# Three token norms run by quarters of the tokens instead of once over all of them

## What is computed

```
h = patches @ W_lin + b + positions                       # class token in front
h = h + recurrent_attention(layernorm(h))                 # layer 0
h = h + bit_linear_ffn(layernorm(h))                      #   8-bit activations, ternary weights
h = h + softmax_attention(layernorm(h))                   # layer 1
h = h + mixture_of_experts(layernorm(h))                  #   32 experts, router picks 8 per token, 2 shared

layernorm(x) = (x - mean(x)) / sqrt(var(x) + 1e-5)        # over the 256 channels, no weights
```

## Time and profile before

| | us |
|---|---|
| median of 3 runs | 880.58 (880.32 to 883.83) |
| profiled execution | 881.1 |
| its span, first to last instruction | 879.4 |
| PE busy in the span | 793.7 (90%) |
| DVE busy | 614.7 (70%) |
| ACT busy | 391.3 (45%) |
| norm 1, from its first mean to the first product behind it | 22.98 to 44.59 |
| norm 2, likewise | 323.96 to 341.19 |
| norm 4, likewise | 526.40 to 542.65 |

### The profile page before, as it was taken

How to read it: one execution, slowest core, us unless ns; L and a number is a source line. 1 busy time by engine, 2 the same in 40 slices (tenths; PEclk the granted TensorE clock), 3 DMA queues, 4 the chain that set the end, 5 groups by cost and what they waited for, 6 DMA issues and landing times.

```text
span 879.4 us, 19821 instructions
## 1 busy us (share of the span) xinstructions
PE 793.7 (90%) x7700; PEld 586.2 (67%) x7700; DVE 614.7 (70%) x976; ACT 391.3 (45%) x561; POOL 183.5 (21%) x197
## 2 busy tenths in 40 slices
PE   4998978989986988977798998799999999999997
PEld 3665757944543666755487885477777777777775
DVE  5796697678787386898767977767777655545544
ACT  5344764610224143666457965334444432323332
POOL 7000790006999801000402420000000000000000
PEclk9999979999999999999999999799999999999999
DMA  8000000020000000010130001144444322222221
GB/s 310 1 2 1 3 1 3 3 96 1 0 0 1 0 2 1 1 39 1 37 78 14 22 21 38 57 127 158 154 150 154 109 68 57 70 69 69 68 61 51
DMA packets 24073, 46.07 MB, mean 52 GB/s; under 512 B 2605, under 2 KB 10541, under 8 KB 23629
## 3 DMA queue, kind: packets, MB, share of 16 engines
q1 hardware_dynamic: 24013, 45.21, 16.8%
HBM read 41.91 MB, written 1.36 MB: 49 GB/s over the span
## 4 chain that ended last, share of the span: by engine, by line
PE 70%; DVE 21%; ACT 4%; issue 3%; POOL 1%; DMA 1%; SPq 0%; DVEq 0%; ACTq 0%; POOLq 0%
PE psum L1790 11%; PE psum L1791 11%; PE psum L1792 11%; PE psum L1982 6%; PE psum L1992 4%; PE psum L828 4%; PE psum L829 4%; PE psum L830 4%; PE psum L2124 1%; DVE arena L1460 1%; PE psum L2170 1%; DVE arena L1658 1%; PE psum L1963 1%; PE psum L2187 1%; PE psum L2156 1%
## 5 line engine op out<-in xcount | busy, mean ns | idle before, releaser
L1790 PE MATMUL psum<-xh,arena 128*128 128x296 f16 (+1 forms) x664 | 193.3, 291 | 8.3 <-DVE xl L1333 5.0
L1791 PE MATMUL psum<-xl,arena 128*128 128x296 f16 (+1 forms) x664 | 193.2, 291 | 0.0
L1792 PE MATMUL psum<-xh,arena 128*128 128x296 f16 (+1 forms) x664 | 193.2, 291 | 0.0
L697 DVE TENSOR_TENSOR arena<-arena 128x592 f16<-128x592 f32 x68 | 52.7, 775 | 61.1 <-ACT arena L608 60.8
L603 ACT ACTIVATE arena<-psum 128x592 f32<-128x592 f32 x66 | 43.8, 664 | 115.7 <-PE psum L1792 115.7
L1790 PEld LDWEIGHTS psum<-xh,arena 128*128 (+2 forms) x664 | 65.3, 98 | 30.8 <-DVE xl L1333 4.5
L752 DVE TENSOR_TENSOR arena<-psum,arena 128x592 f32<-128x592 f32 x64 | 49.6, 775 | 50.8 <-PE psum L1792 50.6
L828 PE MATMUL psum<-arena 128*128 128x296 f16 x272 | 79.9, 294 | 4.6 <-DVE arena L697 3.8
L608 ACT ACTIVATE arena<-arena 128x592 f16<-128x592 f32 x66 | 46.0, 696 | 77.6 <-DVE arena L691 74.8
L829 PE MATMUL psum<-arena 128*128 128x296 f16 x272 | 79.9, 294 | 0.0
L830 PE MATMUL psum<-arena 128*128 128x296 f16 x272 | 79.8, 293 | 0.0
(11 more groups left out here) (321 smaller groups left out, 1675.3 us busy)
## 6 DMA issues: line engine op xcount, KB each, us to landing
arena<-comb SPq DMA_DIRECT2D x62, 296.0 KB, 3.3
arena<-in_wmoe SPq DMA_DIRECT2D x34, 384.0 KB, 3.0
arena<-in_xt SPq DMA_DIRECT2D x4, 864.0 KB, 9.6
arena<-in_w SPq DMA_DIRECT2D x2, 1024.0 KB, 6.6
arena<-arena SPq DMA_DIRECT2D x6, 187.0 KB
arena<-in_ctrl SPq DMA_DIRECT2D x1, 1056.0 KB, 9.1
out<-arena SPq DMA_DIRECT2D x2, 512.0 KB, 3.1
arena<-in_wlin SPq DMA_DIRECT2D x1, 768.0 KB, 4.4
```

What stands on the lines that cost most here:

```text
L697: dve.tensor_tensor(al[:, s_], t1, ah[:, s_], ALU.subtract).then_inc(ev["al"], 1)
L1790: pe.matmul(dst, wh, mh, start=start, stop=False)
L1791: pe.matmul(dst, wh, ml, start=False, stop=False)
L1792: return pe.matmul(dst, wl, mh, start=False, stop=stop)
```

## The change

For ln1, ln2 and ln4 the new `norm_by_quarters` gives each quarter a mean, a variance, a root, a reciprocal and a spreading of its own. In round r the engines do: the product of quarter r, the mean of quarter r-1, the variance of r-2, the spreading of r-3, and (on DVE) the last step of r-4. So a quarter's root and reciprocal run while later quarters are still projected. ln3 keeps the old form.

The tile shapes change. A quarter's 296 sums now lie as 4 rows (`PARTS`) of 74 columns (`PART`) in its own 32 partitions: eight matmuls of 74 columns, each with a slice of `mean_comb` (one column of 1/256 among zeros) that puts its sums into row x. Root and reciprocal are then 32 x 74 (rows 4 to 31 hold zeros from the sums). Spreading takes four matmuls of 74 columns a quarter, with a column of `ident`, broadcast 128 wide, that picks row x.

In the diff the first of the three functions is ACT's, the second DVE's, the third PE's. The 16 fillers before the spreading and, in ln1, the 12 before `condition` are gone; 4 stand before the last spreading in ln2 and ln4. The fillers of the work that follows ln2 (18) and ln4 (12) stay. The small inputs of ln1 go into round 2, the two weight splits of ln4 into round 5.

```diff
+PARTS = 4
+PART = CH // PARTS
...
+            def norm_by_quarters(name, split=True):
+                if name != "ln2":
+                    act.activation(warm[:, int(name[2]) - 1:int(name[2])], eps[:, 0:1], ACT.Sqrt)
+                for r in range(1, NCH + 3):
+                    if 0 <= r - 2 < NCH:
+                        q = r - 2
+                        rows = slice(32 * q, 32 * q + 32)
+                        full(act, (name, "v", q))
+                        act.activation(sd[rows, 0:PART], bank((name, "v", q))[rows, 0:PART], ACT.Sqrt,
+                                       bias=eps[rows, 0:1]).then_inc(emptied["act"], 1)
+                    if r - 1 < NCH:
+                        q = r - 1
+                        after(act, (name, "m", q))
+                        act.activation(sq[:, :, cols(q)], xc[:, :, cols(q)], ACT.Square).then_inc(ev[name + "_sq"], 1)
+                    if 0 <= r - 3 < NCH:
+                        q = r - 3
+                        after(act, (name, "r", q))
+                        if split:
+                            act.activation(xh[:, :, cols(q)], xc[:, :, cols(q)], ACT.Copy).then_inc(ev[name + "_xh"], 1)
...
+            def norm_by_quarters(name, lead, last, extra):
+                for r in range(NCH + 4):
+                    if r < NCH:
+                        lead(r)
+                    if 0 <= r - 1 < NCH:
...
+                        dve.tensor_tensor(xc[:, :, cols(q)], hT[:, :, cols(q)], mean, ALU.subtract).then_inc(emptied["dve"], 1)
+                    if 0 <= r - 2 < NCH:
...
+                        dve.reciprocal(sd[rows, 0:PART], sd[rows, 0:PART]).then_inc(ev[name + "_rec"], 1)
+                    if 0 <= r - 3 < NCH:
...
+                    if 0 <= r - 4 < NCH:
+                        last(r - 4)
+                    if r in extra:
+                        extra[r]()
...
-            norm("ln1", lead=tok_lead, meanwhile=small_inputs)
+            norm_by_quarters("ln1", tok_lead, low_part("ln1"), {2: small_inputs})
...
-            norm("ln4", lead=turned_back, meanwhile=last_lows)
+            norm_by_quarters("ln4", turned_back, low_part("ln4"), {5: last_lows})
...
+            def norm_by_quarters(name, source, lead):
+                for r in range(NCH + 3):
+                    if r < NCH:
+                        lead(r)
+                    if 0 <= r - 1 < NCH:
...
+                    if 0 <= r - 2 < NCH:
+                        q = r - 2
+                        ps = fill((name, "v", q))[32 * q:32 * q + 32, 0:PART]
+                        pe.wait_ge(ev[name + "_sq"], q + 1)
+                        for x in range(PARTS):
+                            comb = mean_comb[:, PARTS - 1 - x:PARTS - 1 - x + 32]
+                            at = CH * q + PART * x
+                            pe.matmul(ps, comb, sq[:, 0, at:at + PART], start=x == 0, stop=False)
+                            ins = pe.matmul(ps, comb, sq[:, 1, at:at + PART], start=False, stop=x == PARTS - 1)
+                        ins.then_inc(filled[who((name, "v", q))], 1)
+                    if 0 <= r - 3 < NCH:
...
+                        if q == NCH - 1 and name != "ln1":
+                            keep_clock(ps, KEEP["quarter"])
+                        pe.wait_ge(ev[name + "_rec"], q + 1)
+                        for x in range(PARTS):
+                            ins = pe.matmul(ps[:, PART * x:PART * x + PART],
+                                            ident[rows, 32 * q + x:32 * q + x + 1].to_broadcast([32, 128]),
+                                            sd[rows, 0:PART], start=True, stop=True)
...
-                if (i, q) == (0, 0):
-                    keep_clock(ps, KEEP["split"])
```

More of the change, by code:

```diff
@@ L104, in norm, with norm_by_quarters @@
             add((name, "r", q), "dve")
-    norm("ln1", lambda q: [add(("tok", c, q), "dve") for c in range(2)])
+    def norm_by_quarters(name, lead):
+        for r in range(NCH + 3):
+            if r < NCH:
+                lead(r)
+            if 0 <= r - 1 < NCH:
+                add((name, "m", r - 1), "dve")
+            if 0 <= r - 2 < NCH:
+                add((name, "v", r - 2), "act")
+            if 0 <= r - 3 < NCH:
+                add((name, "r", r - 3), "dve")
+    norm_by_quarters("ln1", lambda q: [add(("tok", c, q), "dve") for c in range(2)])
     for h in range(2):
@@ L151, in token_max @@
             add((name, "m", n), "act")
-    norm("ln2", lambda q: [add(("op", c, q), "dve") for c in range(2)])
+    norm_by_quarters("ln2", lambda q: [add(("op", c, q), "dve") for c in range(2)])
     token_max("mx1")
@@ L166, in plan_tiles @@
                 add(("v1", n), "dve")
-    norm("ln4", lambda q: [add(("OT", n), "dve") for n in (2 * q, 2 * q + 1)])
+    norm_by_quarters("ln4", lambda q: [add(("OT", n), "dve") for n in (2 * q, 2 * q + 1)])
     add(("lg",), "act")
@@ L277, in tower, with last_in @@
         router_bank = {("lg",): 1, ("cT", 0): 7, ("cT", 1): 0, ("cT", 2): 1}
+        def last_in(b):
+            return [key for key in order[:place[("ln4", "r", 2)][0]] if place[key][0] % 8 == b][-1]
         n0 = place[("f2", 0, 0)][0]
@@ L1089, in _ @@
             act.activation(ctrlh, ctrl_raw, ACT.Copy).then_inc(ev["ctrlh"], 1)
-            norm("ln1")
+            norm_by_quarters("ln1")
             act.wait_ge(ev["dw"], 1)
@@ L1296, in _ @@
                         weight_high(act, e // 2, e % 2, 16 * (e // 2 + 1))
-            norm("ln4")
+            norm_by_quarters("ln4")
             moe_act(act, link)
@@ L1797, in keep_clock @@
                               stop=True)
+            def norm_by_quarters(name, source, lead):
+                for r in range(NCH + 3):
+                    if r < NCH:
+                        lead(r)
+                    if 0 <= r - 1 < NCH:
+                        q = r - 1
+                        after(pe, source(q))
+                        ps = fill((name, "m", q))[:, 0:CH]
+                        pe.matmul(ps, mean_ones[:], hT[:, 0, cols(q)], start=True, stop=False)
+                        pe.matmul(ps, mean_ones[:], hT[:, 1, cols(q)], start=False, stop=True).then_inc(
+                            filled[who((name, "m", q))], 1)
+                    if 0 <= r - 2 < NCH:
+                        q = r - 2
+                        ps = fill((name, "v", q))[32 * q:32 * q + 32, 0:PART]
[6 more added lines that the diff above has]
+                        ins.then_inc(filled[who((name, "v", q))], 1)
+                    if 0 <= r - 3 < NCH:
+                        q = r - 3
+                        rows = slice(32 * q, 32 * q + 32)
+                        ps = fill((name, "r", q))
+                        if q == NCH - 1 and name != "ln1":
[5 more added lines that the diff above has]
+                                            sd[rows, 0:PART], start=True, stop=True)
+                        ins.then_inc(filled[who((name, "r", q))], 1)
             def norm(name, source, lead=None):
@@ L1817, in norm @@
                 ins.then_inc(filled[who((name, "v"))], 1)
-                if name == "ln1":
-                    pe.wait_ge(ev["masks"], 1)
                 keep_clock(fill((name, "r", 0)), KEEP["rec"])
@@ L1838, in tokens @@
                     ins.then_inc(filled[who(("tok", c, q))], 1)
-            norm("ln1", lambda q: ("tok", 1, q), tokens)
+            norm_by_quarters("ln1", lambda q: ("tok", 1, q), tokens)
             pe.wait_ge(ev["condl"], 1)
@@ L2045, in token_max @@
                         ins.then_inc(filled[who((name, kind, n))], 1)
[L2047 removed]
+            norm_by_quarters("ln2", lambda q: ("op", 1, q), out_projection)
             token_max("mx1")
```

34 lines of the change are left out of this document (27 added, 7 removed).

## The result

The changed kernel took 886.39 us (median of 8 runs, 885.50 to 891.04), the kernel before 880.75 on the same chip (8 runs). The ratio is 1.0056, with a 95% interval of 1.0037 to 1.0076. The forecast was 879.4 with a range to 883.6, so the time lies outside it, on the slow side. The profiled execution took 888.99, its span 887.3.

What follows compares the result with a forecast made beforehand. PE was taken to bound the kernel, with 70% of the chain. Norms 1, 2 and 4 at -1.2, +0.5 and -0.4 us made -1.2 with rounding: 881.1 profiled became 879.9, less 0.5 for the median, 879.4 us; range 875.6 to 883.6.

Steps and rivals of the forecast that it cites:

- Norm 1, -1.2 forecast: ln1: PE-bound rounds of 2.9 us, the rotation's second L1416 at about 51.1 instead of 52.28, so -1.2 us.
- the walk: All three norms: PE, DVE and ACT orders followed row by row, each start the later of engine's end and input's hand-over.
- the loop from v2 to v3: Norm 1, sums of squares of quarters 2 to 3: root 2 precedes ACT's square 3, 2.2 us, v3 starting at 40.8.
- Norm 2, +0.5 forecast: ln2: 18 fillers behind the last spreading end last, so the transposes start at 341.67 instead of 341.19, +0.5 us.
- Norm 4, -0.4 forecast: ln4 to the router: Silu starts earlier and L709 starts at 547.9 against 548.33, so -0.4 us.
- Silu 0.4 us earlier: ACT behind norm 4: Silu starts at 545.5 against 545.88, as it no longer waits for `gate_up`.
- Rival 1: Spreading: passes as short as the 74-column transposes, 0.065 instead of 0.11 us, total -3.1, 877.5 us; chance 0.12.
- rival 4: Eight-matmul sums of each quarter: a pass costs a weight load, 0.107 us, total +6.7, 887.3 us; chance 0.10.
- rival 5: Spreading: loads into the same 32 rows stand in the open, 0.17 us a pass, total +2.9, 883.5 us; chance 0.06.
- Rival 2: Behind ln1 or in a norm where fillers went: one more low clock stretch, +1.7 us, 881.1 us; chance 0.18.
- cost nothing: Norm 1: the 28 fillers that go lay beside waits, so their removal was put at no cost.
- masks: Spreading: the wait for `masks` that goes guarded nothing later than DVE's own wait; put at no cost.

Runs made afterwards that it cites:

- ln2_only: Norm 2 alone by quarters, the other norms in the old form with their old fillers, against the kernel before: 887.05 us, ratio 1.0043.
- norm 1 alone: Norm 1 by quarters, norms 2 and 4 in the old form with their old fillers, against the kernel before: 885.15 us, ratio 1.0026.
- the changed kernel on the second chip: The changed kernel, unedited, measured again on another chip against the kernel before there: 886.80 us, ratio 1.0042.

## Why the prediction was wrong

- **Norm 1, -1.2 forecast, +0.2 measured at full clock.** The mechanism (rounds bound by PE, the wait behind the last quarter shorter) is what the rows show. The step that failed is a term that the walk put at nothing: the start of a group of another block. The forecast let PE lose 0.1 only "where PE stood", but PE lost 0.09 to 0.15 at each of the three groups of a round while it was busy, 3.27 instead of 2.90. Mean 2 moved by 1.25 instead of 0.9. A smaller slip: the loop from v2 to v3 was put at 2.2 with a root of 0.27, where the forecast's own root is 0.32; it took 43.86 - 41.43 = 2.43.
- **Norm 2, +0.5 forecast, +2.2 measured.** The same term, on a longer run of groups, twelve changes of block where there were four: PE goes from the sums of quarter 3 through two spreadings, 4 fillers and 18 fillers to the transposes with hardly a stop. That the fillers end last was right, and shown by taking ten away.
- **Norm 4, -0.4 forecast, +0.8 measured.** Again PE without a gap, and twelve changes of block. A second step failed with it: the forecast had Silu 0.4 us earlier "as it no longer waits for `gate_up`". It came 20.6 after the first mean, where it was 19.5 (545.88), and PE's `gate_up` (L1866) was still what it waited for, as before:

```profile
554.25 0.66 ACT L645 ACTIVATE arena<-psum 128x592 f32<-128x592 f32 x1 [0.32 <-PE psum L1866]
```

- **The prices.** Sums 0.066 a pass for 0.064, spreading 0.11 for 0.11, reciprocal 0.61 for 0.62, root 0.31 for 0.32. All right, inside a group. Rival 1 (0.065 a pass for the spreading), rival 4 (0.107 for the sums) and rival 5 (0.17) are refuted by these rows.
- **The spreading's price had been taken without asking what it was before.** The earlier trace rows showed 0.82 us for eight passes of 296 columns, less than the eight times 0.25 that 296 columns take in a mean. That was the sign that loads and matmuls of different 32-row groups run beside each other, which a quarter in its own 32 rows gives up. I put the two numbers side by side and passed on. The sum had the quarters' own price right; what it did not ask is why four of them cost five times what the four had cost together. The Trainium skill (TensorE: Matmul & The Clock Gate, section The mechanism) says that loads overlap matmuls in flight only where the row group differs. The measurements agree in direction: 0.033 a pass into changing groups, 0.11 into one. They differ in size: 0.11 is the load alone, so a load into the same group still hides the 0.06 of the stream, and rival 5's reading was too strict.
- **The clock.** Rival 2 had one more low stretch at +1.7. The changed kernel's low time was 55 us in the mean on two chips, 4.5 above before where both ran beside each other. The rival was right in kind; its 3.4 us more of low time was too little, and its price of one half too much, as over the runs of before 1 us of low time goes with 0.2 to 0.3 us of span. The forecast also said that the fillers that go "cost nothing"; taking such fillers from the old form cost 18 us of low clock and some 4 us of time.
- **`masks`.** The forecast called this wait needless. It guarded the fillers, which read a mask; it could go only because they went.

In sum: 879.4 forecast, 886.4 measured. 4.3 us of the 7.0 are the norms' lengths (+3.2 instead of -1.1). That the changes of block carry most of it is read from the rows: 0.37 a round over the forecast in norm 1, and in norm 2 1.2 us in eleven changes, where the norm is 1.7 over the forecast. No run takes the changes away and keeps the rounds. The other 2.7 fit the longer low time, but this is by remainder: on the chip of the result it is 55.1 in the mean of the changed kernel's 8 runs against 40.4 in the one execution of before whose clock is known. Which places fall to the low clock in a given run was not settled; the stretches at 94 and 316 us, in code that the change does not touch, came and went between kernels. They are no mark of the change: `ln2_only`, whose work up to 316 us is that of before, has them too (0.72 granted over 92 to 104 and 0.83 over 312 to 322, as in the changed kernel; the one profile of before has 0.91 and 1.00).

A version that keeps the rounds and puts a quarter's four rows of sums into four different groups of 32 partitions was not tried. Its four spreadings would write one PSUM bank from different row groups with nothing that orders them, and the Trainium skill (PSUM — Partial Sum Buffer, section PSUM bank collisions raise a hardware error) says that this collides. No run here shows it.

## What to carry to other kernels

Cutting a step into quarters to hide a serial chain pays only if the cut does not make the bounding engine work more: count the groups, not only the passes, and where neighbouring groups use blocks of another size (128*128, 128*32, 32*128), give each its own 0.1 us; a wait that is long over costs nothing. Before moving small matmuls apart, look at what ran side by side when they stood together. If a chain is long because of an elementwise operation over redundant rows, fold the data first (0.6 to 1.0 us a norm here, with the order of the work untouched), and pipeline only if that is not enough.

## What the runs showed of the hardware

- Neighbouring f32 matmuls of 74 columns with 32 x 128 weights start 0.033 us apart when their weights go to other groups of 32 rows in turn (and their results to other banks), and 0.11 apart when all go to the same 32 rows and one bank.
- When a matmul uses a block of another size than the one before it, its load is not run ahead and it starts 0.09 to 0.14 us behind the end of the stream before it, with or without a wait; behind the same block most start within 0.02 us of it, those with a wait too (four in five of 346).
- Sums with 128 x 32 weights and 74 columns start 0.066 apart a pass, the streaming time of the columns, though all loads go to the same 128 rows.
- The low clock's price is far below one half: over the 33 to 35 runs of before on each chip the span rises by 0.2 to 0.3 us for each us at the low level. That much of the low time lies where PE is not the bound would explain it; no run shows it.
- PE busy for 2.20 of 7 us was followed by a low clock, and so, in two profiles, were 6.8 of 7 us mostly in small f32 matmuls, while in a third 6.56 of 7 were not (norm 1 alone, above). One of the two:

```profile
38.00:45.00 7.00, 6.82 (x70) 1.00 0.01 4
45.00:53.00 8.00, 7.73 (x38) 0.57 0.00 0
```

This is the changed kernel on the second chip. PE's busy share alone does not tell whether the clock stays up.
